# Expert weights issued ahead of the later slot lists, rows gathered four blocks ahead, and two latent exponentials moved in an attention and mixture-of-experts kernel

## The reference

```
xn  = layernorm(x)
s   = latent attention(xn)        # 16 heads, 16 + 64 rotary dimensions, causal; then @ w_out.T
h   = xn + ordinary attention(rmsnorm(xn, w_ln1))   # 16 heads of 16, causal
t   = rmsnorm(h, w_ln2)
logits = t @ Wr.T                  # 8 experts
top_logits, top_idx = top_k(logits, 2); probs = softmax(top_logits)
y_e = (silu(t @ Wg[e].T) * (t @ Wu[e].T)) @ Wd[e].T   # inner width 512
ffn = h + sum over the two chosen experts of probs * y_e
out = x + s * silu(ffn)
```

## Time and profile before

| | |
|---|---|
| median of 3 runs | 926.57 us (924.39 to 929.02) |
| the profiled execution | 925.26 us, of which the span in the trace 922.7 us |
| PE busy | 824.1 us (89%) |
| DVE / ACT / POOL busy | 613.2 / 501.9 / 388.2 us |
| granted clock, mean | 0.952 |
| attention stage | 0 to about 650 us |
| routing of the last batch, first lists and gathers | about 650 to 672 us |
| 23 expert blocks | about 672 to 898 us |
| last scatter, read back, result | about 898 to 922.7 us |

### The profile page before, as it was taken

How to read it: one execution, slowest core, us unless ns; L and a number is a source line. 1 busy time by engine, 2 the same in 40 slices (tenths; PEclk the granted TensorE clock), 3 DMA queues, 4 the chain that set the end, 5 groups by cost and what they waited for, 6 DMA issues and landing times.

```text
span 922.7 us, 18329 instructions
## 1 busy us (share of the span) xinstructions
PE 824.1 (89%) x6432; PEld 734.0 (80%) x6432; DVE 613.2 (66%) x2207; ACT 501.9 (54%) x1089; POOL 388.2 (42%) x538
## 2 busy tenths in 40 slices
PE   5889999999998998999899899878478999999990
PEld 3877988887897896898788789656367999999980
DVE  4876667666757766767666675762536878787754
ACT  2445365366456446637536545635136878787761
POOL 5532342344343344234434334415324565657541
PEclk9888999999999999999999999988688999999995
DMA  9000000000000000000000000124239999999936
GB/s 283 1 1 2 14 1 14 13 12 3 25 13 2 25 14 2 25 14 1 14 14 13 3 24 12 18 77 131 55 65 286 239 224 240 244 255 241 230 39 193
DMA packets 49868, 71.04 MB, mean 77 GB/s; under 512 B 12066, under 2 KB 36002, under 8 KB 49762
## 3 DMA queue, kind: packets, MB, share of 16 engines
q1 hardware_dynamic: 39058, 57.40, 20.4%
q0 software_dynamic: 9856, 12.13, 7.6%
q10 hardware_dynamic: 864, 0.36, 0.2%
HBM read 55.12 MB, written 14.81 MB: 76 GB/s over the span
## 4 chain that ended last, share of the span: by engine, by line
PE 60%; DMA 12%; issue 10%; DVE 8%; POOL 5%; ACT 4%; another core or an unknown queue 0%; SPq 0%; POOLq 0%; ACTq 0%; DVEq 0%
PE ps L595 47%; DMA expert_rows<-yo,slot_of 10%; PE ps L689 6%; PE ps L726 3%; POOL expert_rows L572 3%; DVE ps L1496 2%; ACT ex L1160 2%; PE ps L622 2%; DVE ps L1493 1%; POOL xg L561 1%; DMA w_ukv_raw<-in_w_ukv 1%; PE ps L631 1%; DMA xg<-x_normalised,slot_of 1%; DVE xr L1781 1%; DVE s_tok L1779 1%
## 5 line engine op out<-in xcount | busy, mean ns | idle before, releaser
L531 POOL TENSOR_SCALAR_AFFINE_SELECT ex<-ex 128x256 f32<-128x256 f32 x256 | 106.5, 419 | 244.5 <-ACT ex L1160 221.2
L595 PE MATMUL ps<-qt,kt 128*128 128x256 f32 (+1 forms) x768 | 164.1, 327 | 5.9 <-issue 2.4
L1160 ACT ACTIVATE ex<-ps 128x384 f32<-128x384 f32 x240 | 116.9, 497 | 92.3 <-PE ps L595 90.3
L509 POOL TENSOR_TENSOR tok<-tok,swp 128x256 f32<-128x256 f32 x128 | 97.5, 762 | 114.6 <-DVE swp L1458 113.6
L1493 DVE CUSTOM_DVE_ANT_0 ps<-ps,mask 128x128 f32<-128x128 f32 x256 | 76.5, 299 | 87.3 <-PE ps L595 82.6
L595 PEld LDWEIGHTS ps<-qt,kt 128*128 128x128 f32 x768 | 109.2, 194 | 17.5 <-issue 6.4
L1496 DVE CUSTOM_DVE_ANT_0 ps<-ps,mask 128x256 f32<-128x256 f32 x256 | 118.5, 463 | 0.0
L572 POOL DMA_INDIRECT expert_rows<-yo,slot_of x46 | 75.5, 1641 | 94.4 <-ACT yo L1294 76.9
L1331 DVE TENSOR_TENSOR wel<-raw,weh 128x768 fp32r<-128x768 f32 x92 | 87.7, 956 | 25.7 <-ACT weh L1030 18.4
L595 PE MATMUL ps<-wh,xth 128*128 128x320 f32 (+2 forms) x352 | 95.6, 354 | 3.7 <-DVE wl L1331 2.8
L1454 DVE TENSOR_TENSOR tok<-ps,cos_t 128x320 f32<-128x320 f32 x128 | 62.8, 491 | 52.8 <-PE ps L595 52.1
(11 more groups left out here) (164 smaller groups left out, 1902.2 us busy)
## 6 DMA issues: line engine op xcount, KB each, us to landing
raw<-in_w_experts SPq DMA_DIRECT2D x92, 384.0 KB
mla_branch<-s_b SPq DMA_DIRECT2D x8, 256.0 KB, 2.1
expert_rows<-xn SPq DMA_DIRECT2D x8, 256.0 KB, 2.1
x_normalised<-otk SPq DMA_DIRECT2D x8, 256.0 KB, 2.1
xr<-in_x SPq DMA_DIRECT2D x1, 2048.0 KB
s_tok<-mla_branch SPq DMA_DIRECT2D x4, 512.0 KB
w_cols_raw<-in_w_cols SPq DMA_DIRECT2D x1, 1792.0 KB, 15.4
x<-expert_rows SPq DMA_DIRECT2D x3, 512.0 KB, 5.1
```

The source lines that it names most:

```text
L509: nc.gpsimd.tensor_tensor(t, t, swp[:, n % 2, :, :], ALU.add).then_inc(tokd, 1)
L531: nc.gpsimd.affine_select(a, a, [[0, 2], [1, P]], ALU.is_ge, zero, 0, -1).then_inc(exm, 1)
L595: return nc.tensor.matmul(o, a, m, start=start, stop=stop, skip_group_check=True, **k)
L1160: nc.scalar.activation(ex[:, h % (2 * G), :], ps[4 + h % 2][:, P:4 * P], ACT.Exp, scale=scale).then_inc(ex_, 1)
```

## The change

Three edits.

1. SP issues the weights of block 2 right behind the eight static lists (and the wait for the block map), then the store of the last batch's latent branch, then three later lists, the weights of block 3, three more lists, and so on; the last three lists stand behind the weights of block 6.
2. POOL gathers blocks 0 to 3 ahead of its loop, and block b+4 in turn b.
3. In ACT's last batch exponentials 0, 1 and 2 stand ahead of `keep_back` and `keep_v2`, which stood behind exponential 0.

```diff
             sp.wait_ge(msc, 64 * B)
             for e in range(NSTAT):
                 load_slots(e, slot[e * REGION:e * REGION + BS, :])
+            def later_lists(j0, j1):
+                for j in range(j0, j1):
+                    row = sp.value_load(bmap[0:1, 1, j:j + 1], min_val=0, max_val=SLOTS - BS)
+                    load_slots(NSTAT + j, slot[bass.ds(row, BS), :])
+
             sp.wait_ge(bmapd, 1)
-            for j in range(NDYN):
-                row = sp.value_load(bmap[0:1, 1, j:j + 1], min_val=0, max_val=SLOTS - BS)
-                load_slots(NSTAT + j, slot[bass.ds(row, BS), :])
-            store_s(last)
             for blk in range(2, NB):
                 if blk < NSTAT:
                     load(blk, w_experts[blk, :, :])
...
+                if blk == 2:
+                    store_s(last)
+                if blk < 7:
+                    later_lists(3 * (blk - 2), 3 * (blk - 1))
...
-            for blk in range(NXG - 1):
+            for blk in range(NXG):
                 gather(blk)
             for blk in range(NB):
-                if blk + NXG - 1 < NB:
-                    gather(blk + NXG - 1)
+                if blk + NXG < NB:
+                    gather(blk + NXG)
                 scatter(blk)
...
                 act.wait_ge(pv2, NG * b)
-                latent_exp(0)
+                for h in range(3):
+                    latent_exp(h)
                 keep_back(b - 1, fb2, of2, o2)
                 keep_v2(b)
-                for h in range(1, 2 * G):
+                for h in range(3, 2 * G):
                     latent_exp(h)
```

## The result

The changed kernel took 912.28 us (median of 4 runs, 911.51 to 917.78) against 925.78 us (4 runs) of the kernel before; the ratio is 0.9857, with a 95% interval of 0.9814 to 0.9900. Forecast were 914.2 us, in a range of 911.0 to 918.0. The profiled execution took 912.69 us, 12.6 us less than that of before, and its span is 911.0 us, 11.7 less.

What follows compares the result with a forecast made beforehand. The prediction took PE to bound the kernel, with a stop and half clock at the expert stage's entry. Its terms, 8.4 + 3.1 + 1.4 - 0.5 = 12.4 us, took 926.57 to 914.2 us, range 911.0 to 918.0.

Steps and rivals of the forecast that it cites:

- What bounds the kernel: Whole kernel: mostly PE; at the expert stage's entry a stop from SP's late weight issue, then half clock, then PE-bound.
- The stop, 8.4 us: Block 2's weights issued 20.8 us sooner end PE's 5.8 us idle and save 2.6 us of half clock.
- The lists behind the weights, nothing: Fifteen later lists moved behind weights: gather 8 first wants them, the delay lies in slack, cost nothing.
- Rival D: Slower: late lists hold gather 8 and scatter 4, then ACT and PE; 930.6 us at 35 us late; chance 0.03.
- Gathers, 3.1 us: Late expert blocks: gathering one block earlier ends three PE waits for rows, worth 3.1 us, bounds 0 to 3.1.
- Rival A: From 800 us on, scatters hold the stretch, so earlier gathers bring nothing; 917.3 us; chance 0.10.
- Exponentials, 1.4 us: Last batch: exponentials 1 and 2 ahead of `keep_back` start latent head 3 sooner, 1.4 us, bounds 0 to about 2.
- The collision, 0.5 us: First gathers beside block 2's weights: block 0's second gather loses 0.5 us, bounds 0 to 2.6; block 1's nothing.
- the shared 0.9 us: Last part of block 0's second gather, shared with block 2's weights; if doubled, the cost is 0.9 instead of 0.5 us.
- Rival C: At block 2 the stop stays its size through another late ACT input; about 922.1 us; chance 0.06.
- Rival B: First gathers: the collision with block 2's weights costs its full 2.6 us; 916.2 us; chance 0.08.
- The sum: Whole kernel: 8.4 + 3.1 + 1.4 - 0.5 = 12.4 us, median from 926.57 to 914.2 us.

Runs made afterwards that it cites:

- b1_before: The kernel before, unchanged, run again for its trace on another chip; ratio 0.9983 to the kernel before.
- x1_exps: The kernel before with only the exponentials 0, 1 and 2 of the last batch moved ahead of `keep_back`; ratio 0.9971 to the kernel before.
- x3_gather: The kernel before with only the rows gathered one block earlier; ratio 0.9945 to the kernel before.
- x5_no_sp: The changed kernel without its first edit: SP's order as before, gathers earlier and exponentials moved; ratio 0.9937 to the kernel before.
- s1_early_read: The kernel before with the four 512 KB reads of the latent branch issued eight blocks earlier; ratio 1.0010 to the kernel before.
- after: First trace of the changed kernel, all three edits against the kernel before, on the first chip; median 912.28 us, ratio 0.9857.
- before: First trace of the kernel before, without the three edits, on the first chip; median 925.78 us.
- h2_hold: The changed kernel with block 2's weights held until PE has transposed block 1, run beside the changed kernel; ratio 0.9910 to the kernel before.
- h1_hold: The changed kernel with block 2's weights held until PE has transposed block 1, without the changed kernel beside it; ratio 0.9866 to the kernel before.
- a1_after: The changed kernel, all three edits, run again on another chip; ratio 0.9889 to the kernel before.

## Why the prediction was right, point by point

**What bounds the kernel.** Right: the stop lay in SP's order, and moving the issue of one block's weights ended it.

**The stop, 8.4 us.** 8.25 in the first pair of traces, of which one is the trace that it was read from. The split into idle time and half clock holds too (b1_before: 3.65 + 1.65). But the term is not the kernel's: it was 3.6 to 5.3 us in five traces on other chips (x1_exps, x3_gather, b1_before, x5_no_sp, s1_early_read), and the two pauses of SP had lengthened it. The price of a list, 1.35 us, was a mean over those pauses and the 1.2 us between the eighth list and the first later one; without them it is 1.14. The median of the first chip can't tell how often such pauses come.

**The lists behind the weights, nothing.** Right: no wait for a list but the first, no wait for weights. Rival D, in which lists hold gather 8 and with it the scatters, didn't occur.

**Gathers, 3.1 us.** 3.9 in the first pair, of which one is the trace that the term was read from. In the five traces without the edit on other chips it is 2.5 to 6.7, and it goes entirely; so one trace tells this term no better than that. Rival A, that scatters would hold the stretch, is refuted by x3_gather. I had put it down to the DMA engines' load in general; s1_early_read shows that the four reads do most of it.

**Exponentials, 1.4 us.** About 1.5 at half clock, as in the trace that the term was read from, and 1.7 at full clock; PE's idle time there is 1.56 us where the clock is full. The other 1.4 us of the first pair were the clock's chance.

**The collision, 0.5 us.** The size is about right, the place wrong. I let it fall on block 0's second gather and took block 1's for covered, by the 5.5 us of a late gather. The time from the first list to block 0's transposes didn't change (6.26 us before, 6.31 after), and block 1's rows came 0.3 to 0.8 us late. The step that failed is the bound: 5.5 us was what a gather took beside a stream of weights that waits for its buffers. In after, block 1's second gather, issued at 669.22, took 6.7 us beside four quarters issued at once. The Trainium skill ("DMA: Bandwidth & Descriptors", section "Queues, rings and completion order") has the DMA engines take turns between queue rows, a packet at a time, and by it the prediction doubled the shared 0.9 us of block 0's second gather; no run shows that doubling, since block 0's time grew by 0.05 us.

**Rival C**, a stop that stays under another name, is refuted by all traces with the first edit.

**Small slips in the prices.** Rival B comes to 916.3 us and not 916.2, and rival D at 35 us late to 930.2 and not 930.6; nothing hangs on either.

**The sum.** 12.4 us forecast, 13.5 between the medians and 12.6 between the profiled executions. As a ratio 0.9867 was forecast; 0.9857 was measured on the first chip, 0.9889 and 0.9881 on two others, 10 to 11 us, where the stop is smaller. The mechanisms were right, but that the number is so near is in part luck. Between the first two traces the last batch gave 3.1 us instead of 1.4, and the late gathers 3.9 instead of 3.1. Against that the first blocks lost 2.0 us instead of 0.5, and another 1.4 us went ahead of them (0.71 up to latent head 0, 0.68 between latent head 3 and the first transposes).

## What to carry to other kernels

When an engine waits for a transfer, look at what the issuing queue did just before: here fifteen small loads that nobody needed for eight blocks stood ahead of the one that was needed next, and where SP had no pauses moving it ahead of the last three of them was enough. A term read from one trace is that execution's; before it is carried further, check by a second trace whether a pause or a half clock in it comes every time. A prefetch one step deeper cost nothing on the queue here and covered disturbances whose source need not be known. But a transfer that is issued earlier meets other traffic: block 2's weights, issued at the lists, met the first gathers (0.3 to 0.8 us), and issued ahead of them they met the slots (3.8 us).

## What the runs showed of the hardware

- After 2.3 us of idle time in block 1 (x1_exps) TensorE's granted clock stayed at 1.00, the 2.4 GHz level; after 3.21 us (x5_no_sp), 3.65 us (b1_before) and 5.8 us (before) it fell to 0.50 (1.2 GHz), and the next 3 to 5 us of work took twice as long. So idle time alone doesn't decide it: in the last batch it fell around an idle time of only 1.16 us in five of fourteen traces, in one execution of a kernel and not in another (h2_hold and h1_hold).
- Behind the idle time at the entry of the expert stage the clock rose 6.4 to 8.4 us after the first transposes in thirteen traces, and 11.0 us after them in a1_after. PE had been idle there for 0.61 us at block 1's rows, in the others for 0.28 at most.
- A gather of 256 rows in two DMAs took from the issue of the second to its use 2.9 us with no weights beside it (before, DMA share 0.51), 5.5 us beside the stream of weights (before), and 6.7 us beside the four quarters of block 2 issued at once (after).
- SP issued a list behind a load of its address from SBUF every 1.14 us, against 0.51 for a list with a fixed address. Single ones took 2.8 us, and 4.3 in after, on the first chip.
- The same kernel took 925.8 us on one chip and 908 us on three others.
